# Scatter of rows to two experts: one wide row per token tile instead of a row slot per choice, with the loops written out

## What is computed

```python
def _L1_ffn_ref(x, gate_w, gate_b, w1, b1, w2, b2, ws1, bs1, ws2, bs2):   # x: the normalised rows
    logits = xf @ gate_w + gate_b
    top_w, top_i = jax.lax.top_k(logits, 2)
    gw = jax.nn.softmax(top_w, axis=-1)
    combine = (gw[:, :, None] * jax.nn.one_hot(top_i, 8)).sum(axis=1)
    for e in range(8):
        h = gelu(xf @ w1[e] + b1[e])
        out = out + combine[:, e:e + 1] * (h @ w2[e] + b2[e])
    shared = gelu(xf @ ws1 + bs1) @ ws2 + bs2
    return out + shared
```

## Time and profile before

| | us |
|---|---|
| median of 3 runs (3393.05 to 3399.75) | 3397.09 |
| profiled execution, its own time | 3396.84 |
| its span, first to last instruction | 3395.0 |

### The profile page before, as it was taken

One profiled execution on the slowest core, in us unless ns is written; L12 is line 12 of the kernel. 1 busy time (PEld: TensorE's weight loads), 2 busy tenths in 40 slices (PEclk: granted clock), 3 DMA queues, 4 the chain that ended last, 5 costly groups with the idle time before them and its releaser, 6 DMA issues. The chain is left out here.

```text
span 3395.0 us, 71130 instructions
## 1 busy us (share of the span) xinstructions
PE 2554.7 (75%) x19941; PEld 1860.1 (55%) x19941; DVE 2189.5 (64%) x4872; ACT 1594.0 (47%) x3527; POOL 776.3 (23%) x1113
## 2 busy tenths in 40 slices
PE   3657759999897566999459999966567999972370
PEld 1334543459787333999237777766444666651260
DVE  5967875237687423776856666556977888863267
ACT  2545513332364233776636666632254777750253
POOL 0001100000000365555422222200151222203553
PEclk7899859999998688999679999958787999975695
DMA  3093000111371011222685555300095556500123
GB/s 99 0 253 100 31 13 23 32 45 51 63 122 56 29 43 47 70 69 63 212 184 70 69 68 68 47 1 0 0 262 66 69 69 75 72 33 23 59 76 104
DMA packets 316132, 240.86 MB, mean 71 GB/s; under 512 B 27068, under 2 KB 297836, under 8 KB 315692
## 3 DMA queue, kind: packets, MB, share of 16 engines
q1 hardware_dynamic: 288248, 202.91, 30.4%
q0 software_dynamic: 19072, 28.28, 2.9%
q10 hardware_dynamic: 8704, 8.39, 0.9%
HBM read 139.83 MB, written 96.51 MB: 70 GB/s over the span
## 5 line engine op out<-in xcount | busy, mean ns | idle before, releaser
L2562 ACT ACTIVATE h_pt<-h_ps 128x384 f32<-128x384 f32 (+1 forms) x1024 | 543.0, 544 | 279.1 <-PE h_ps L2471 143.8
L2311 DVE TENSOR_REDUCE h_nm<-h_ps 128x4 f32<-128x1024 f32 (+1 forms) x448 | 540.0, 1219 | 158.3 <-PE h_ps L2442 62.1
L1846 POOL DMA_INDIRECT results<-e_y,e_ykey x208 | 212.3, 1021 | 191.0 <-DVE e_y L1835 171.2
L1803 DVE TENSOR_SCALAR e_wt<-w 128x1156 f32 (+1 forms) x208 | 140.9, 678 | 174.6 <-PEq L1583 89.5
L2490 PE MATMUL h_ps_o<-h_pt,h_vp 128*32 128x256 f32 (+1 forms) x4096 | 246.8, 359 | 1.3 <-ACT h_pt L2562 1.3
L1893 ACT ACTIVATE e_hid<-e_ps_h,e_wt 128x128 f32<-128x128 f32 x688 | 201.9, 369 | 21.9 <-PE e_ps_h L1867 14.3
L1867 PE MATMUL e_ps_h<-e_hT,e_wt 128*128 128x128 f32 x1376 | 197.4, 284 | 14.5 <-ACT e_hT L1888 7.9
L1875 PE MATMUL e_ps_o<-e_wt,e_hid 128*128 128x128 f32 x1376 | 194.9, 280 | 8.5 <-ACT e_hid L1893 4.9
L2476 PE MATMUL h_ps<-h_sq,h_sk 128*128 128x256 bf16 x1024 | 193.8, 275 | 9.2 <-ACT h_pt L2562 4.4
L1656 POOL DMA_INDIRECT sorted_rows<-e_row,e_pos x128 | 123.2, 963 | 301.4 <-DVE e_row L1635 243.8
L2413 PE MATMUL h_ps<-h_sk,h_sq 128*128 128x256 bf16 x1024 | 160.9, 282 | 37.8 <-DVE h_identb L2293 35.5
(11 more groups left out here) (449 smaller groups left out, 6283.5 us busy)
## 6 DMA issues: line engine op xcount, KB each, us to landing
h_sk<-k_stack SPq DMA_DIRECT2D x192, 128.0 KB
q_stack<-p_parts SPq DMA_DIRECT2D x64, 256.0 KB, 3.3
h_sq<-q_stack SPq DMA_DIRECT2D x64, 256.0 KB
sorted_rows<-pad SPq DMA_DIRECT2D x26, 520.0 KB, 11.6
e_xt<-sorted_rows SPq DMA_DIRECT2D x104, 130.0 KB
e_got<-results SPq DMA_DIRECT2D x24, 512.0 KB, 5.1
k_stack<-p_parts SPq DMA_DIRECT2D x32, 384.0 KB, 3.2
b_tz<-ktab SPq DMA_DIRECT2D x32, 256.0 KB, 7.1
```

What stands on the lines that cost most here:

```text
L1803: dve.tensor_scalar(wt[j % 4][:, :], w[:, :, :].rearrange("p e w -> p (e w)")[:, ds(at, wc)], 1.0, None, ALU.mult).then_inc(e_w.sem, 1)
L1846: gp.indirect_dma_start(ys[:, :], bass.IndirectOffsetOnAxis(ap=key[m // 4][:, m % 4:m % 4 + 1], axis=0), y[m][:, :], None).then_inc(return ...
L2311: dve.tensor_reduce(to, got, AX, ALU.max, negate=True).then_inc(s["mx"].sem, 1)
L2562: act.activation(pt[g % 2][:, j, :], ps_2[:, h % 2, 0:SW], ACT.Exp, scale=scale).then_inc(s["ex"].sem, 1)
```

## The change

The two choices of a token get one and the same row: weight of choice 0, token number, 128 normalised features, weight of choice 1, and the offset of choice 0's expert, 132 numbers. All 64 tiles of these wide rows lie in SBUF (`wide_rows`), so there are no slots and no waits for them; DVE writes 64 rows instead of 128, ACT copies no numbers, and POOL sends each row tile twice, to the two places. In the expert loop a row no longer says which choice it is: DVE compares the offset in the row with that of the tile's own expert (`placef`), five small operations for every four tiles. The loops of the scatter block are written out; DVE's order is now four units of rows first, then for each unit `added_of(u)` and the rows of unit u+4; PE's is hidden(u+1), turn_back(u-1), project(u); ACT's is hidden_kept(u+1), out_kept(u). The pad rows get the new layout; `e3` keeps its rows of 130 numbers.

```diff
+        xs1 = nc.dram_tensor("sorted_wide_rows", (tiles_of(2) * P, D + 4), F32).ap()
...
                     for n, (choices, _) in enumerate(rows_of):
-                        gp.memset(pad[n][:, :, 0:D + 1], 0.0)
-                        ins = gp.memset(pad[n][:, :, D + 1:D + 2], float(spare_of(choices)))
-                    ins.then_inc(padded, 1)
+                        gp.memset(pad[n][:, :, :], 0.0).then_inc(padded, 1)
+                    gp.wait_ge(padded, 3)
+                    for n, (choices, _) in enumerate(rows_of):
+                        at = 1 if choices == 2 else D + 1
+                        gp.memset(pad[n][:, :, at:at + 1], float(spare_of(choices) - (choices - 1) * NB * SEQ)).then_inc(padded, 1)
+                    gp.memset(pad[0][:, :, D + 3:D + 4], -1.0).then_inc(padded, 1)
...
-                                link(dve, dve.tensor_copy(meta[:, k, :, 0], weight[k]))
-                                link(dve, dve.tensor_scalar(meta[:, k, :, 1], c("tvec", 0, NT), first_row[:, :],
-                                                            float(k * NB * SEQ), ALU.add, ALU.add))
+                                link(dve, dve.tensor_copy(meta[k][:, :, 0], weight[k]))
+                            link(dve, dve.tensor_scalar(meta[0][:, :, 1], c("tvec", 0, NT), first_row[:, :], None, ALU.add))
+                            if choices == 2:
+                                numbers = c("tvec", 0, n_exp).unsqueeze(1).to_broadcast([P, NT, n_exp])
+                                link(dve, dve.tensor_tensor(tot[:, :, :], sel[0], numbers, ALU.mult))
+                                link(dve, dve.tensor_reduce(posf[:, :], tot[:, :, :], AX, ALU.add))
+                                link(dve, dve.tensor_scalar(meta[1][:, :, 1], posf[:, :], float(wc), None, ALU.mult))
...
+                                def rows_of_unit(u):
+                                    for tile in range(u * UT, (u + 1) * UT):
+                                        dve.tensor_scalar(wide_rows[:, tile, 2:2 + D], src[:, tile, :], mean[:, tile:tile + 1],
+                                                          rstd[:, tile:tile + 1], ALU.subtract, ALU.mult).then_inc(g_row.sem, 1)
...
+                                for u in range(4):
+                                    rows_of_unit(u)
+                                for u in range(NU):
+                                    added_of(u)
+                                    if u + 4 < NU:
+                                        rows_of_unit(u + 4)
...
-                                        gp.wait_ge(*g_row.now(i, n + 1))
-                                        gp.wait_ge(*g_meta.now(i, n + 1))
-                                        gp.indirect_dma_start(xs[:, :], bass.IndirectOffsetOnAxis(
-                                            ap=pos[:, n % choices, tile:tile + 1], axis=0), row[n % ROWS][:, :], None
-                                            ).then_inc(sent[n % ROWS], 16)
+                                for n in range(NT * choices):
+                                    tile, k = divmod(n, choices)
+                                    if k == 0:
+                                        gp.wait_ge(*g_row.now(tile // per, tile % per + 1))
+                                    gp.indirect_dma_start(xs[:, :], bass.IndirectOffsetOnAxis(
+                                        ap=pos[:, k, tile:tile + 1], axis=0), wide_rows[:, tile, :], None
+                                        ).then_inc(sent[n % ROWS], 16)
...
+                                hidden_kept(0)
+                                for u in range(NU):
+                                    if u + 1 < NU:
+                                        hidden_kept(u + 1)
+                                    out_kept(u)
...
+                                hidden(0)
+                                for u in range(NU):
+                                    if u + 1 < NU:
+                                        hidden(u + 1)
+                                    if u:
+                                        turn_back(u - 1)
+                                    project(u)
+                                turn_back(NU - 1)
...
+                                    if choices == 2:
+                                        first_w, token, second_w, first_at = (xt[:, four, i] for i in (0, 1, D + 2, D + 3))
+                                        dve.tensor_tensor(second[:, four], first_at, placef[:, ds(n + 1, 4)], ALU.not_equal
+                                                          ).then_inc(e_sum.sem, 1)
+                                        dve.wait_ge(*e_sum.now(rm, 5 * g + 1))
+                                        dve.scalar_tensor_tensor(to, second[:, four], float(NB * SEQ), token, ALU.mult, ALU.add
+                                                                 ).then_inc(e_sum.sem, 1)
+                                        dve.tensor_tensor(wb[:, four], second[:, four], second_w, ALU.mult).then_inc(e_sum.sem, 1)
+                                        dve.scalar_tensor_tensor(wa[:, four], second[:, four], 0.5, first_w, ALU.is_lt, ALU.mult
+                                                                 ).then_inc(e_sum.sem, 1)
+                                        dve.wait_ge(*e_sum.now(rm, 5 * g + 4))
+                                        dve.tensor_tensor(row_w[:, four], wa[:, four], wb[:, four], ALU.add).then_inc(e_sum.sem, 1)
+                                        dve.wait_ge(*e_sum.now(rm, 5 * g + 5))
                                     dve.wait_ge(*e_key.now(rm, g - 1))
                                     dve.scalar_tensor_tensor(empty[g][:, :], to, float(spare),
...
-                                    dve.tensor_scalar(y[m][:, :], y[m][:, :], xt[:, m, D:D + 1], None,
+                                    dve.tensor_scalar(y[m][:, :], y[m][:, :], row_w[:, m:m + 1], None,
                                                       ALU.mult).then_inc(e_y.sem, 1)
...
-                                    pe.transpose(ps_t[:, m % 2, 0:P], xt[:, m, 0:D], ident).then_inc(e_t.sem, 1)
+                                    pe.transpose(ps_t[:, m % 2, 0:P], xt[:, m, X0:X0 + D], ident).then_inc(e_t.sem, 1)
```

204 lines of the change are left out of this document (81 added, 123 removed).

## The result

| | before | changed |
|---|---|---|
| median of 8 executions each, in turn (us) | 3395.51 | 3411.67 |
| range (us) | 3392.1 to 3401.9 | 3404.5 to 3418.1 |
| profiled execution, its own time (us) | 3396.84 | 3404.49 |
| its span (us) | 3395.0 | 3402.2 |

The changed kernel is slower: ratio 1.0045, 95% interval 1.0031 to 1.0060, where 3383 us was forecast. Its profiled execution is the shortest of the eight, so the trace shows 7.7 of the 16 us; up to `collect`, where all edits are behind, it shows 13.7.

What follows compares the result with a forecast made beforehand. No engine was full in the scatter block, POOL coming nearest; PE bounded the expert loop. 3396.8 + 1.4 - 30.1 - 0.6 - 1.5 + 17 gave 3383 us; range 3366 to 3436, the forecast's own 3372 to 3397.

Steps and rivals of the forecast that it cites:

- POOL at 1.263 us throughout, -30.1: Scatter block: POOL's 128 scatters run without stops, 161.4 us instead of 191.5, saving 30.1 us.
- The others in the block: "117 us, well under 161": Scatter block: PE needs 7.3 us a unit, 117 us for 16 units, below POOL's 161.
- rival A: Scatter block: PE's words stay late, a unit takes lateness L + 4.7; 3443 us, middling course 3415; chance 0.37.
- The block's end, -1.5: Scatter block's end: PE is done earlier and only the last landing is left, saving 1.5 us (bounds 0.7 and 2.5).
- Table +1.4: Table block: DVE's chain gains a product, a reduction and a scaling and loses one 64-wide operation, adding 1.4 us.
- first scatter -0.6: Scatter block's start: the first scatter needs only the first row, saving 0.6 us (bounds 0 and 1.1).
- Loops written out, 0: Scatter block: branches cost PE's queue 0.2 us, seven times, off the path, so writing out the loops changes nothing.
- pads, 0: Attention stage: twice the memsets and 1.5% more bytes stay hidden, 0 us, or +1 without that cover.
- Expert loop, +17: Expert loop: DVE's five operations cost 0.77 us a group less 0.23 slack, 34 groups, +18, less 1 for two tiles' lead.
- B: Expert loop: DVE's additions eat the gain, +31 against -31, 3397 us; chance 0.12.
- C: Expert loop: DVE's additions are free, 0 to 3 us in all, 3368 us; chance 0.09.
- D: Clock: PE idles and starts the expert loop at the lower level, as it does now, costing nothing new.

Runs made afterwards that it cites:

- rows_first_2: Changed kernel with DVE writing all 64 rows before its first addition; 3479.7 us, single run, beside the kernel before at 3397.1.
- drain_8_2: Changed kernel with POOL waiting before every eighth scatter of the scatter block until all earlier ones have landed; 3407.6 us, single run, kernel before 3399.9.
- deep_break_8: deep_slots_2's text, with POOL waiting before every eighth of its first 80 scatters for the preceding scatter's landing; 3386.1 us, 0.9970 of the kernel before.
- three_ops: Changed kernel with the choice costing DVE three operations per four tiles instead of five; 3406.9 us, 1.0038 of the kernel before.
- short_break_8: As deep_break_8, but POOL waits only for the landing of the scatter before the last one; 3399.2 us, 1.0008 of the kernel before.
- deep_slots_2: Changed kernel's orders, but two numbers for each choice again, 32 slots written by DVE, old expert loop; 3404.0 us, 1.0012 of the kernel before.

## Why the prediction was wrong, step by step

**POOL at 1.263 us throughout, -30.1: wrong, -8.9.** This is the step that failed. Its reasoning was that 40 us of rows in store bridge late words of 9 us. It took the lateness of the earlier trace rows as a fixed delay. But the lateness depends on how long POOL has scattered without a stop. In the kernel before POOL runs dry every 24 us or so, because it has only eight slots, and the word is there 2.5 us after the last scatter. A deeper store makes the runs longer: in the changed kernel the first hole comes after 40 scatters, DVE gets its word 4.5 us after the last of them (1199.97, 1204.50), and that word was 25.5 us late (`turn_back` had ended at 1178.99). In rows_first_2, with no stop at all, ACT is up to 50 us late. So the delay grew with the cover. That breaks of 2.1 us prevent it is shown (drain_8_2, deep_break_8); that POOL's own stops end a phase that has begun is argued from these times.

**The others in the block: "117 us, well under 161": wrong.** PE's units took (1340.2 - 1165.6) / 15 = 11.6 us each. ACT's bias began on average 4.8 us behind the project (77 us over 16 units, from the timeline), so rival A's formula L + 4.7 gives 9.5; it left out that the four words of `hidden` are late as well (ACT e_hs waits 21.1 us for a DMA that isn't its own and 12.7 us for "remote", together 2.1 a unit).

**The block's end, -1.5: wrong, +5.3,** for the same reason: PE is the last now, not the landing.

**Rival A is what happened.** Its middling course gave 3415; the median is 3411.7. What it had against it, ten scatters in the first step with ACT prompt, was read as evidence that scatters don't matter; it was the time ahead of the onset, before some 15 scatters in a row. The argument against the loops, that the last `turn_back` is late outside them, was in the text and should have weighed more. The Trainium skill, page "Runtime: NRT & Kernel Launch", section "Instruction fetch mechanics", would have put the lateness on the taken branches; with the branches gone it stayed, so that rule doesn't explain this trace.

**Table +1.4 and first scatter -0.6: right.** From the table block's first copy to DVE's first row it is 18.33 us (1130.62 to 1148.95) instead of 16.84 (1129.76 to 1146.60), +1.5, and the first scatter follows that row by 0.65 us instead of 1.77, -1.1. The chain began 0.86 us later already, which makes up the +1.2. **Loops written out, 0; pads, 0:** not contradicted.

**Expert loop, +17: right (+16.1), by two errors that cancel.** One group in the changed kernel:

```profile
1466.08 0.16 DVE L1805 TENSOR_TENSOR e_second<-e_xt,e_placef 128x4 f32<-128x4 f32 x1
...
1466.62 0.16 DVE L1814 TENSOR_TENSOR e_chosen_w<-e_wa,e_wb 128x4 f32<-128x4 f32 x1
1467.03 0.16 DVE L1817 SCALAR_TENSOR_TENSOR e_empty<-e_chosen_to,pack 128x4 f32<-128x4 f32 x1 [0.24 <-DVE e_chosen_w L1814]
1467.34 0.17 DVE L1824 TENSOR_TENSOR e_ykey<-e_empty,e_chosen_to 128x4 int32<-128x4 f32 x1
1467.46 0.29 DVE L1830 TENSOR_TENSOR e_y<-e_ps_o,e_wt 128x128 f32<-128x128 f32 x1
...
1469.11 0.28 DVE L1830 TENSOR_TENSOR e_y<-e_ps_o,e_wt 128x128 f32<-128x128 f32 x1
```

From the first operation to the key pair it is 0.95 us, not 0.77: the last wait costs 0.41, not 0.19. The key pair itself has become longer too, 0.43 us to the next bias instead of 0.29, so a group costs 1.38 - 0.29 = 1.09 us more. And a cycle without a group takes 1.65 us, not 1.76: in the 1.76 of the earlier trace rows DVE was also waiting for PE (its weight copy stood 0.48 us, in the changed kernel 0.35), which the prediction allowed for only in its bound of 0.6. The slack can be worked out from the rates. The result scatters come each 271.6/135 = 2.012 us, 8.05 for four tiles; less the 1.09 DVE would take 6.96, against PE's 4 x 255.5/135 = 7.57. The slack was 0.61 us, not 0.23, and 1.09 - 0.61 = 0.48 is what 16.1/34 = 0.47 us a group shows. three_ops agrees: its group costs 1.11 - 0.29 = 0.82 us more (1465.49 to 1466.60 in its timeline), less 0.61 and times 34 that is 7 us, measured 8.6.

**Rivals B, C, D.** B (+31) and C (0 to 3) lie on either side of the measured +16.1. D, the clock, cost nothing new: from 1343 to 1347 us its granted value is 0.57 in the changed kernel and 0.50 before.

Behind `collect` the profiled execution wins back 6.5 us in stages that no edit touches. The shortest of eight executions is one reason to expect that; which stages vary, and why, wasn't settled.

## What to carry to other kernels

A wait whose length nobody can explain is not a constant that a buffer can bridge: before counting on a deeper store, find out what ends the wait, because the stop that the buffer removes may be what ends it. Where a rate is held by a queue of small operations, measure that engine's cycle where it runs freely, and count the wait behind the last of the added operations as well. And profile the kernel before on more than one chip: here the whole gain aimed at existed on only one of two sorts.

## What the runs showed of the hardware

- On some chips or occasions PE's words to ACT and DVE come late while POOL's indirect scatters follow each other at 1.263 us, from some 15 scatters on. They do come while POOL runs, 1.5 to 50 us late, the later the longer POOL has run (ACT's longest single wait is 33.6 us, in rows_first_2), and after 128 scatters without a stop they stayed late for 17.6 us more. A pause of 2.1 us after every eight scatters prevents it (drain_8_2: no late word), 0.8 us doesn't (short_break_8: 74.2 us).
- This happens in three of five groups of runs (kernel before at 3397 to 3400 us) and not at all in two (3358 us), with the same text. Each group was one chip, so chip and occasion can't be told apart. The first comparison, with the kernel before at 3395.5 us, is of the late sort.
- What in the chip holds the words back stays open. The runs show only when it begins and what prevents it. The Trainium skill, page "Perfetto Trace Analysis", section "Tensor Engine Instruction (MATMUL, LD_WEIGHTS)", says that the end shown for a TensorE instruction is estimated and that its semaphore update is pushed only when PSUM has acknowledged the written bytes; by that page a late acknowledgement would look just like these rows. No run here separates it from a late word. A scatter's own times hardly differ: 958 ns at the median in both sorts, 962 in rows_first_2, deep_slots_2 and the two kernels with short breaks.
